# Attention heads paired across two key groups, one key product for four pairs of heads

## The reference, cut to what matters

```python
Q = (X @ Wq).reshape(n, s, 4, 4, 64)      # groups, heads per group, width
K = (X @ Wk).reshape(n, s, 4, 64)
V = (X @ Wv).reshape(n, s, 4, 64)
raw = einsum('bsgwe,btge->bstgw', Q, K * scale)
attn = softmax(raw, axis=2)
A = einsum('bstgw,btge->bsgwe', attn, V).reshape(n, s, 1024)
return X + A @ Wpost
```

## Time and profile before

| | |
|---|---|
| runs, us | 2687.07, 2688.45, 2696.65 |
| median, us | 2688.45 |
| profiled execution, us | 2689.84 |
| its span, first to last instruction, us | 2687.7 |
| PE matmul busy | 2259.2 us, 84% |
| DVE busy | 1847.3 us, 69% |
| ACT busy | 1772.0 us, 66% |
| GpSimd busy | 1737.7 us, 65% |
| granted clock of PE, mean | 0.945 of full speed |

### The profile page before, as it was taken

How to read it: one execution, slowest core, us unless ns; L and a number is a source line. 1 busy time by engine, 2 the same in 40 slices (tenths; PEclk the granted TensorE clock), 3 DMA queues, 4 the chain that set the end, 5 groups by cost and what they waited for, 6 DMA issues and landing times.

```text
span 2687.7 us, 38166 instructions
## 1 busy us (share of the span) xinstructions
PE 2259.2 (84%) x13155; PEld 1413.0 (53%) x13192; DVE 1847.3 (69%) x2832; ACT 1772.0 (66%) x3282; POOL 1737.7 (65%) x1416
## 2 busy tenths in 40 slices
PE   5777989999688989888989898989889979988761
PEld 4444567775454556445655465456445645554441
DVE  5778555543347876786667767776677666879888
ACT  3556633446278777878677867786778668756862
POOL 1000255416768898878798789887977797656566
PEclk9888989999899999999999999999999989999895
DMA  4000278874566667655764485447534854477776
GB/s 160 24 20 5 89 192 235 233 207 82 92 133 124 119 148 167 121 106 111 173 121 98 102 187 114 96 108 178 113 80 88 189 111 90 87 163 165 177 168 152
DMA packets 282033, 344.50 MB, mean 128 GB/s; under 512 B 66160, under 2 KB 211505, under 8 KB 281841
## 3 DMA queue, kind: packets, MB, share of 16 engines
q0 software_dynamic: 84080, 175.67, 35.0%
q1 hardware_dynamic: 175248, 144.83, 18.7%
q10 hardware_dynamic: 22512, 21.57, 2.4%
HBM read 198.26 MB, written 26.80 MB: 84 GB/s over the span
## 4 chain that ended last, share of the span: by engine, by line
POOL 27%; issue 15%; PE 15%; ACT 8%; DVE 7%; DMA 1%; POOLq 0%; another core or an unknown queue 0%; DVEq 0%; ACTq 0%
POOL arena L1661 11%; POOL acc_sb L1639 8%; POOL arena L1667 4%; POOL arena L1677 4%; DVE bank L1536 3%; PE bank L1944 2%; PE bank L1913 2%; PE bank L1786 2%; PE bank L1739 2%; PE bank L1779 2%; DMA x<-in_X 1%; PE bank L1798 1%; ACT bank L1160 1%; PE bank L1836 1%; ACT Pr L1043 1%
## 5 line engine op out<-in xcount | busy, mean ns | idle before, releaser
L1661 POOL TENSOR_TENSOR arena<-arena 128x512 f32<-128x512 f32 x512 | 872.6, 1781 | 17.1 <-DVE arena L1527 17.1
L1252 DVE TENSOR_REDUCE negmax<-bank 128x1 f32<-128x512 f32 x512 | 341.0, 681 | 260.7 <-PE bank L1779 260.2
L1639 POOL DMA_INDIRECT acc_sb<-ybuf,slot_idx x256 | 421.0, 1645 | 126.1 <-DMA ybuf<-arena 61.4
L1160 ACT ACTIVATE bank<-arena,A_sb 128x512 f32<-128x512 f32 x512 | 353.1, 694 | 160.4 <-DVE arena L1541 134.3
L1667 POOL TENSOR_TENSOR arena<-arena 128x512 f32<-128x512 f32 x192 | 295.6, 1540 | 230.9 <-DVE arena L1536 230.4
L1536 DVE TENSOR_TENSOR_SCAN bank<-bank,arena 128x512 f32<-128x512 f32 x320 | 390.4, 1220 | 73.9 <-ACT bank L1160 39.3
L1043 ACT ACTIVATE Pr<-bank,negmax 128x512 f32<-128x512 f32 x512 | 359.5, 702 | 115.6 <-DVE negmax L1252 115.4
L1786 PE MATMUL bank<-ident,Pr 128*128 128x128 f32 x2048 | 341.0, 291 | 70.5 <-ACT PT L1025 70.0
L1025 ACT COPY PT<-bank 128x512 f32<-128x512 f32 x512 | 304.1, 594 | 142.2 <-PE bank L1786 127.4
L1786 PEld LDWEIGHTS bank<-ident,Pr 128*128 128x128 f32 x2048 | 229.3, 145 | 309.3 <-ACT PT L1025 179.5
L1677 POOL DMA_DIRECT2D arena<-arena x255 | 279.7, 1097 | 121.5 <-DVE arena L1541 121.2
(11 more groups left out here) (215 smaller groups left out, 3710.9 us busy)
## 6 DMA issues: line engine op xcount, KB each, us to landing
arena<-arena POOLq DMA_DIRECT2D x255, 512.0 KB, 5.3
arena<-bc_dram SPq DMA_DIRECT2D x256, 256.0 KB, 3.8
ybuf<-arena ACTq DMA_DIRECT2D x64, 256.0 KB, 4.6
arena<-in_w_gate SPq DMA_DIRECT2D x64, 128.0 KB, 3.0
arena<-in_w_up SPq DMA_DIRECT2D x64, 128.0 KB, 4.2
arena<-in_w_down SPq DMA_DIRECT2D x64, 128.0 KB, 4.9
arena<-in_X SPq DMA_DIRECT2D x8, 512.0 KB, 8.4
s_sb<-in_X SPq DMA_DIRECT2D x8, 512.0 KB, 6.4
```

Of the source, the lines that this page charges most:

```text
L1160: act.activation(bank[DECAY[g % 2]][:, :], dt_sb[:, size_slot(b, cb), :], ACT.Exp, scale=A_sb[:, cb, n:n + 1]).then_inc(ssm_decay, 1)
L1252: dve.tensor_reduce(negmax[:, m % RING_STAT:m % RING_STAT + 1], bank[m % RING_S_ATT][:, :], AX.X, ALU.max, negate=True).then_inc(att_max, 1)
L1639: pool.indirect_dma_start(acc_sb[:, i, :], None, ybuf, bass.IndirectOffsetOnAxis(ap=slot_idx[:, b * TILES + i, k:k + 1], axis=0), bounds_c ...
L1661: pool.tensor_tensor(st_sb[:, g % RING_S, :], u_sb[:, size_slot(b, cb), :], B_sb[:, load % RING_BC, :], ALU.mult).then_inc(ssm_input, 1)
```

## The change

The pairs are now made of heads of two groups: pair p holds head p % 4 of group 2t and head p % 4 of group 2t+1, where t = `twin(p)` = p // 4. The host permutes the columns of Wq and the rows of Wpost to match (`paired`). `Wk_sb` holds each group once, and a slice of 128 columns gives the keys of group 2t in the lower half and of group 2t+1 in the upper half, so that one key product serves four pairs. Two key products are left in a batch: the first, and one at n = 25 (pair 3). The scores read `Kp` of the twin, and `values` takes for each head the V columns of its own group. The key weights are loaded by one transfer, and `W_ATT` counts four loads.

```diff
+TWINS = GROUPS // 2
-    Wk_sb = sb("Wk_sb", [P, KC, GROUPS * 2 * HD])
+    Wk_sb = sb("Wk_sb", [P, KC, GROUPS * HD])
-    W_FIRST, W_SMALL, W_ATT, W_SSM = 16 * 5, 16 * 7, 16 * 7, 16 * 4
+    W_FIRST, W_SMALL, W_ATT, W_SSM = 16 * 5, 16 * 7, 16 * 4, 16 * 4
+    def twin(p):
+        return p // HPG
 ...
             def loads(self):
-                for c in range(KC):
-                    for half in range(2):
-                        dst = Wk_sb[:, c, :].rearrange("p (g t d) -> p g t d", t=2, d=HD)[:, :, half, :]
-                        act.dma_start(dst, Wk[c * P:(c + 1) * P, :].rearrange("p (g d) -> p g d", d=HD)).then_inc(w_att, 16)
-                for dst, src in ((Wq_sb, Wq), (Wv_sb, Wv), (Wpost_sb, Wpost)):
+                for dst, src in ((Wk_sb, Wk), (Wq_sb, Wq), (Wv_sb, Wv), (Wpost_sb, Wpost)):
                     act.dma_start(dst[:, :, :], src.rearrange("(c p) n -> p c n", p=P)).then_inc(w_att, 16)
 ...
-            def copy_k(self, b, g, bk):
-                w.wait_ge(att_kmm, GROUPS * b + g + 1)
-                w.wait_ge(att_scored, ATT_STEPS // GROUPS * (GROUPS * b + g - 1))
-                act.activation(Kp[:, g % 2, :], bank[bk][:, :], ACT.Copy, scale=HD ** -0.5).then_inc(att_k, 1)
+            def copy_k(self, b, t, bk):
+                w.wait_ge(att_kmm, TWINS * b + t + 1)
+                w.wait_ge(att_scored, ATT_STEPS // TWINS * (TWINS * b + t - 1))
+                act.activation(Kp[:, t % 2, :], bank[bk][:, :], ACT.Copy, scale=HD ** -0.5).then_inc(att_k, 1)
 ...
-                if at == K_AT and p + 1 < PAIRS and p % 2:
-                    self.copy_k(b, (p + 1) // 2, spare(n))
+                if at == K_AT and p + 1 < PAIRS and twin(p + 1) > twin(p):
+                    self.copy_k(b, twin(p + 1), spare(n))
 ...
-                if at > K_AT and pair % 2 and pair + 1 < PAIRS:
-                    w.wait_ge(att_k, GROUPS * b + (pair + 1) // 2 + 1)
+                if at > K_AT and pair + 1 < PAIRS and twin(pair + 1) > twin(pair):
+                    w.wait_ge(att_k, TWINS * b + twin(pair + 1) + 1)
 ...
-                    pe.matmul(bank[m % RING_S_ATT][:, :], Qp[own, p % 2, i * P:(i + 1) * P], Kp[own, p // 2 % 2, :], start=True, stop=True).then_inc(att_scored, 1)
+                    pe.matmul(bank[m % RING_S_ATT][:, :], Qp[own, p % 2, i * P:(i + 1) * P], Kp[own, twin(p) % 2, :], start=True, stop=True).then_inc(att_scored, 1)
 ...
-                g = p // 2
                 for c in range(TILES):
                     for j in range(2):
+                        g = 2 * twin(p) + j
 ...
-                if at == K_AT and p + 1 < PAIRS and p % 2:
-                    self.product_k(b, (p + 1) // 2, n)
+                if at == K_AT and p + 1 < PAIRS and twin(p + 1) > twin(p):
+                    self.product_k(b, twin(p + 1), n)
 ...
+    paired = np.arange(HEADS * HD).reshape(TWINS, 2, HPG, HD).transpose(0, 2, 1, 3).reshape(-1)
 ...
-        "X": d["L0_attn_X"], "Wq": d["L0_attn_Wq"], "Wk": d["L0_attn_Wk"], "Wv": d["L0_attn_Wv"], "Wpost": d["L0_attn_Wpost"],
+        "X": d["L0_attn_X"], "Wq": d["L0_attn_Wq"][:, paired], "Wk": d["L0_attn_Wk"], "Wv": d["L0_attn_Wv"], "Wpost": d["L0_attn_Wpost"][paired],
```

More of the change, by code:

```diff
@@ L1740, in product, with product_k @@
                 return ins
-            def product_k(self, b, g, n):
+            def product_k(self, b, t, n):
                 w.wait_ge(att_exp, b * ATT_STEPS + n - 1)
-                self.product(Wk_sb[:, :, g * P:(g + 1) * P], spare(n)).then_inc(att_kmm, 1)
+                self.product(Wk_sb[:, :, t * P:(t + 1) * P], spare(n)).then_inc(att_kmm, 1)
             def product_q(self, b, p, n):
@@ L1776, in score @@
                     w.wait_ge(att_q, PAIRS * b + p + 1)
-                    w.wait_ge(att_k, GROUPS * b + p // 2 + 1)
+                    w.wait_ge(att_k, TWINS * b + twin(p) + 1)
                     own = slice(j * HD, (j + 1) * HD)
-                    pe.matmul(bank[m % RING_S_ATT][:, :], Qp[own, p % 2, i * P:(i + 1) * P], Kp[own, p // 2 % 2, :], start=True, stop=True).then_inc(att_scored, 1)
+                    pe.matmul(bank[m % RING_S_ATT][:, :], Qp[own, p % 2, i * P:(i + 1) * P], Kp[own, twin(p) % 2, :], start=True, stop=True).then_inc(att_scored, 1)
             def turn_p(self, b, m):
```

## The result

| | before | changed |
|---|---|---|
| median of 12 runs | 2688.89 us (2687.07 to 2696.65) | 2677.74 us (2673.64 to 2686.28) |
| ratio | | 0.9957 [0.9948, 0.9967] |
| profiled execution, its span | 2689.84 us, 2687.7 us | 2678.76 us, 2676.6 us |
| mean granted clock of it | 0.945 | 0.943 |

What follows compares the result with a forecast made beforehand. PE, 89% busy beside the scan, was taken as nearest its limit, though not everywhere. Terms 10.4 + 1.8 + 1.8 + 0.7 = 14.7 us off the 2688.45 us median gave 2673.7, said as 2674; range 2658 to 2687 us.

Steps and rivals of the forecast that it cites:

- Sites beside the scan: Twelve removed products in batches 2 to 7, each worth 0.87 us from comparing intervals with and without one: 10.4 us.
- the prediction's upper bound: For the twelve products beside the scan: 1.71 us each, as in batch 1 where PE is wholly full, 20.5 us.
- PE as the bound: Rival, 20%: PE bounds the kernel throughout, so 27.3 us go, 2661 us; freed intervals fall to 19.6 us.
- the scan takes it all back: Rival, 26%: only early sites and loads count, 4.3 us, 2684 us; freed intervals stay near 21.3 us.
- The clock rival: Rival, 4%: without the dense products PE is granted 1.2 GHz more often; seven added rounds make it slower, 2702 us.
- The prediction's sign of this rival: A granted clock under 0.9 in several intervals would mean that PE's lower clock takes the gain.
- the prediction's round: A product, two turns, a set of values and a score at the low clock cost 4.0 us more.
- Site 318 us: Second product of batch 1, at the expert stage's start: 3.7 us less 1.9 given back, 1.8 us; ends 0 and 3.7.
- the give-back of 1.9 us: At early low-clock sites, values, a turn and a score run slow in the product's place: 0.9 + 0.4 + 0.6 us.
- Site 78 us: Second product of batch 0, at low clock, DVE waiting 2.39 us for the score behind: 1.8 us; ends 0 and 2.4.
- Sites 623 and 180 us: Fourth products of batches 1 and 0, hidden by GpSimd's gathers and DVE's routing: 0 us each, up to 1.7 and 2.7.
- The loads: At the start, four key loads become one: 0.7 us gain from 262 KB less; ends +2.1 and -2.1 us.

Runs made afterwards that it cites:

- the kernel with the product alone: Changed kernel plus 16 needless key products on PE at the removed places, without ACT copy or wait: 2688.62 us, 0.9995 of the kernel before.
- the unused tile: Changed kernel with one unused 128x512 float tile declared behind Kp, no instruction different: 2688.81 us, 0.9941; when repeated 2689.88 us, 0.9945.
- the third series: Runs on one chip, repeating the changed kernel (2687.59 us, 0.9929) and variants against their own runs of the kernel before (2707.52 us).
- the needless copies: Changed kernel plus 16 needless ACT copies at the removed places and the next score's wait, no product: 2670.86 us, 0.9929; when repeated 2681.9 us, 0.9907.
- the first series: Runs on one chip, with the changed kernel (2677.74 us, 0.9957) and variants against their own runs of the kernel before (2688.88 us).
- The old loads: Changed kernel with the earlier key loads, four 128 KB transfers in 256-byte pieces, two into a spare tile: 2677.76 us, 0.9957 of the kernel before.
- the second series: Runs on one chip, with an unused tile added to the changed kernel as the reference (2688.81 us), against their own runs of the kernel before (2704.1 us).
- 64 products: Changed kernel with 48 needless key products added, with copies and waits, at six steps of each batch: 2732.01 us, 1.0101 of the kernel before.
- with 8: Changed kernel with one key product a batch, keys of groups 2 and 3 left out, no unused tile: 2684.36 us, 0.9919 of the kernel before.

## Why the forecast held, and where its steps did not

**Sites beside the scan: 10.4 us forecast, 11.3 measured, by other numbers.** The step took the difference of the two kinds of stretch, 0.87 us, for what a site would lose. The sites lost 1.39 us; the test of the prediction, about 20.5 us a stretch, was missed (19.98), and PE as the bound (19.6) is missed too. The 1.39 us lie nearer to the 1.71 of the prediction's upper bound than to its 0.87. Then 4.5 us came back in the 18 neighbours, and 2.2 us outside the 36 stretches. The step that failed is that the other kind of stretch shows what is left when a product goes. A stretch without a product is also another part of the scan's order, and its length depends on the clock and on single instructions such as DVE's long one: the two kinds differ by 0.87 us in the kernel before and by 0.00 in the kernel with the product alone, which has as many products and takes as long. The give-back is not the scan evening out a lateness either, for 13 of 18 neighbours keep their length. That 0.87 us is nevertheless near to what the kernel got for each product, 0.90 us between 16 and 64, is in part luck. With the means of the profiled executions (1524.0 us with 32 products, from before and the product alone; 1514.7 us with 16) the 12 sites gave 9.3 us, or 0.78 us each. Over the whole kernel the three series give 0.70 us (11.15/16), 0.96 (15.3/16, with the unused tile) and 1.24 us (19.9/16) for each product. And the kernel with the product alone shows that it is PE's time that is paid for, not ACT's copy or the wait. The two do not simply add, however: between kernels without the copies the 16 products cost 10.9 us (2688.62 and 2677.74), between kernels with them 18.0 us (2688.88 and 2670.86), 1.13 us each.

**The rivals.** PE as the bound throughout is out: it wanted 27.3 us. That the scan takes it all back is out too: it wanted 21.3 us a stretch and 4.3 us in all. Both stay out in the third series too, where 19.9 us [15.2, 23.3] were gained.

**The clock rival, named at 4%, did happen in part**, inside the forecast instead of against it. In the neighbours before, one of 18 showed a clock under 0.97; now three do, the two shown above and one of 22.00 us at 0.92. Of the 12 one does, as before, and of the 6 none, where one did: 4 of 36 now, 3 before. The prediction's sign of this rival, several stretches under 0.9, is absent in this profile, but not in others of a kernel with 16 products: the changed kernel in the third series has one at 0.81 and one at 0.87. What a fall costs shows at the stretch of 22.00 us. PE of the changed kernel there, and PE at the same step with the needless copies:

```profile
2278.67 0.65 PE L1787 MATMUL bank<-ident,Pr 128*128 128x128 f32 x4 [1.90 <-ACT PT L1026]
...
2280.05 1.97 PE L1799 MATMUL bank<-PT,V_sb 128*64 128x128 f32 x16
2281.96 1.11 PE L1787 MATMUL bank<-ident,Pr 128*128 128x128 f32 x4
```

```profile
2271.68 0.66 PE L1799 MATMUL bank<-ident,Pr 128*128 128x128 f32 x4 [1.90 <-ACT PT L1034]
...
2273.01 1.09 PE L1811 MATMUL bank<-PT,V_sb 128*64 128x128 f32 x16
2274.04 0.66 PE L1799 MATMUL bank<-ident,Pr 128*128 128x128 f32 x4
```

Both have the same wait of 1.90 us ahead. After it the values take 1.97 us in the one, the 1.2 GHz level, and 1.09 in the other; the stretch takes 22.00 us against 19.97. That is some 2 us here. The kernel with copies had its low clock (0.93) in the stretch before, so the two differ also in what came earlier. The changed kernel's PE had gaps of 0.62 us (2266.80), 0.59, 0.50 and 0.19 us ahead of the 1.90; the other one 0.40, 0.50 and 0.19 us.

Another pair shows the 4.0 us of the prediction's round, and that the gaps of the stretch alone do not decide. It is the stretch that took 23.21 us before and 24.06 in the changed kernel, in the third series: first the changed kernel, then the one with copies.

```profile
1490.73:1517.94 27.21, 22.23 (x126) 11.93 (x128) 16.91 (x20) 21.66 (x43) 19.19 (x15) 0.81 0.39 87
...
1506.77 1.09 PE L1807 MATMUL bank<-ident,rowinv 128*128 128x128 f32 x4 [1.59 <-ACT Pr L1044]
1507.79 1.98 PE L1799 MATMUL bank<-PT,V_sb 128*64 128x128 f32 x16
```

```profile
1486.99:1510.20 23.21, 18.09 (x126) 9.66 (x128) 16.51 (x20) 21.36 (x42) 16.40 (x13) 1.00 0.36 76
...
1503.02 0.63 PE L1819 MATMUL bank<-ident,rowinv 128*128 128x128 f32 x4 [1.59 <-ACT Pr L1054]
1503.58 1.09 PE L1811 MATMUL bank<-PT,V_sb 128*64 128x128 f32 x16
```

In this stretch PE's waits up to this point are the same in both to 0.01 us (0.32, 1.87, 0.19, 1.02 and 1.59 us in the first), and only in the first does the clock fall, for 4.0 us in all. The changed kernel of the first series, with the same instructions as in the third, took 24.06 us at 0.93. So the cost of the fall differs between executions of one program, 0.9 and 4.0 us here. The Trainium skill, "TensorE: Matmul & The Clock Gate", section "HAM oscillation — how this bites in real kernels", says that repeated waits between groups of matmuls put the array back to half rate. The traces agree in direction, for both falls shown stand behind such waits; neither the page nor they tell why the same waits do it in one execution and not in another.

**Site 318 us: 1.8 us forecast, 3.9 measured.** The stretch with the product took 22.00 us before (308.50 to 330.50) and 18.12 now. The step that failed is the give-back of 1.9 us: with the product gone the clock is at 2.4 GHz there. **Site 78 us: 1.8 forecast, 0.4 measured**: there the give-back did come, in full, and more; the granted clock of the stretch is 0.71, where it was 0.81 before. **Sites 623 and 180 us**: 1.71 us at the first, swallowed by the gathers as forecast, and 0.45 us at the second, forecast at 0. The four stretches in the changed kernel, in order of time, and the first work after each of the two low-clock sites:

```profile
60.22:95.28 35.06, 23.72 (x147) 15.24 (x150) 29.54 (x92) 14.65 (x31) 2.42 (x4) 0.71 0.08 23
172.84:207.25 34.41, 19.74 (x123) 11.25 (x126) 31.53 (x83) 11.76 (x27) 0.00 (x0) 0.80 0.04 8
311.51:329.63 18.12, 16.12 (x186) 9.57 (x188) 10.19 (x20) 12.77 (x29) 10.59 (x8) 1.00 0.81 259
616.67:631.91 15.24, 15.24 (x122) 9.04 (x124) 5.92 (x10) 11.62 (x27) 10.89 (x7) 1.00 0.42 62
...
80.98 1.09 PE L1787 MATMUL bank<-ident,Pr 128*128 128x128 f32 x4 [3.76 <-ACT PT L1026]
...
82.00 2.08 PE L1780 MATMUL bank<-Kp,Qp 64*128 64x512 f32 x4
...
319.12 1.09 PE L1799 MATMUL bank<-PT,V_sb 128*64 128x128 f32 x16
```

At 78 us a turn of 1.09 and a score of 2.08 us are the 1.2 GHz level of the earlier trace rows and above it; at 318 us the values at 1.09 are the 2.4 GHz level.

**The loads: 0.7 us of gain forecast, 2.0 us of loss at the first query copy** (45.0 to 47.0 us), the end of the range that the prediction kept. Two rows of the start of the changed kernel:

```profile
1.28 0.50 ACTq L932 DMA_DIRECT2D Wq_sb<-in_Wq  x1
...
2.37 0.83 ACTq L932 DMA_DIRECT2D Wpost_sb<-in_Wpost  x1
```

The key load is one issue instead of four that took 2.74 us, and so the three large loads stand among the transfers of X. The mis-sized term was the bytes: 262 KB less counted for less than the order. The order is not all of the 2.0 us, however. The old loads give back 2.4 of the 2.7 us at the second tile of X, but only 0.6 at the first query copy; where the other 1.4 us come from is open, with a single profile of before. At the end the loads are worth nothing measurable, as the kernel with the old ones shows.

**Where the early gains went.** The prediction wanted the expert stage's first transpose near 329 us, 4.3 us sooner. It came at 332.20, 0.9 us sooner:

```profile
320.52 1.28 POOL L1631 DMA_INDIRECT arena<-rows,arena  x1 [2.33 <-issue]
...
332.20 0.66 PE L1876 MATMUL bank<-ident,arena 128*128 128x128 f32 x4
```

GpSimd's chain of gathers that leads up to it started 3.0 us later than before (317.51). The lag was 2.0 us at the first query copy, 1.5 at the end of the stretch of site 78 and 3.4 at the start of that of site 180, so more was lost between these two, at places that were not traced. The 3.9 us of site 318 made up for it and left 0.9. From there the lead is 1.3 us at the last gather of rows and 0.0 at the first gather of line 1640, 619.06 us against 619.1:

```profile
L1640 POOL DMA_INDIRECT acc_sb<-ybuf,slot_idx x32: 1539/1548/1604, 619.1 to 676.6; - x32
...
ACT L1074: 11.3, 1
```

The length of the gathers is unchanged and ACT's wait for the last grew from 8.9 us to 11.3: what attention gains beside them is lost, as the prediction said. That the profile shows nothing of the early sites and the medians of the second series 5.9 us is no contradiction. The first gather comes anywhere from 612.8 to 620.2 us in the profiles of the first series, and before is a single profile of this. The changed kernel and before differ by 20 us in the third series and 11 in the first, and I can't say why; the kernel before was not profiled there. What can be said is where the changed kernel is slower in the third series: its first gather comes at 629.9 us instead of 619.1, and from the first query copy of batch 2 on its profile is only 3.8 us longer. So what differs most between the two series lies before 620 us.

## What to carry to other kernels

Where stretches with and without an operation alternate, the difference of their lengths is a weak price for the operation: it was 0.87 us here with a standard error of 0.6, and 0.00 in a kernel that ought to give the same. Before using it, compare the stretches one by one, with their clocks, and look for single instructions of odd length. Work taken from the fullest engine of four that are at 73 to 89% was worth 0.70 to 1.24 of its 1.98 us here, by the series it was measured in. A small shift elsewhere can take part of it back at one place, as DVE's instruction of 4.67 us did. When issues on a queue become fewer, read what now goes out earlier, and what it stands in front of.

## What the runs showed that was not expected

**Stretches at the low clock go with both the products and the copies.** Of the 36 stretches of batches 2 to 7, those with a granted clock of 0.97 or less are, where a copy stands at the sites, 1 with 64 products, 3 with 32 (before) and 2 or 3 with 16; where none does, 5 with 32 (the product alone), 4 to 6 with 16 and 9 with 8. So from 32 to 16 products it is the copies that tell, and only the ends show the products. In the second series the mean granted clock over whole runs is 0.9485 with 64, 0.943 with 32 (before), 0.942 with 16 and 0.9365 with 8. Whether a product less is worth less the fewer are left is open: 0.90 us above 16 and 0.56 below can't be told apart.

**The same kernel scatters with its clock.** The 12 runs of the changed kernel go from 2673.64 us at a mean granted clock of 0.946 to 2686.28 us at 0.933, about 9.3 us for each 0.01 (correlation -0.91). Its 12.6 us of scatter are as large as the gain. With the unused tile one run of 12 took 2716.57 us at 0.901. The kernel before scatters over 9.6 us and hardly with its clock (correlation -0.31 in the 17 runs of the first series, 0.03 in those of the third).

**Needless copies on ACT made the kernel 5.7 to 6.9 us faster**, in two series. Some 5.6 us of it can be placed: 2.1 us in batch 7, at DVE's long instruction; 1.2 us behind the last query copy, not traced further; and 2.3 us elsewhere beside the scan, where fewer stretches are at a low clock with the copies (2 or 3 of the 36, against 4 to 6 without). The stretch of 23.21 us alone takes 23.2 us in all three profiles with copies and 23.2 to 27.2 in the six without. That is shown as going together; why the copies keep the clock up is not shown. The copies seem to help by where they put other instructions in time; if so, another change of a few tenths of a microsecond may undo it.
